# A two-layer sequence kernel on one core: the scaling of expert results moved to ScalarE, one expert's weight splitting spread over the first expert stage, and the choice of experts moved within a range

## The reference, cut to what matters

```
x = layernorm(x + L0_attn(x))      # 16 heads of 8, band |i-j| <= 16, softmax; plus residual
x = layernorm(x + L0_ffn(x))       # 16 experts 128->512->128, gelu, the 4 best by logits, softmax weights
x = layernorm(x + L1_attn(x))      # linear attention: decayed causal sum, reads @ W_read.T
x = layernorm(x + L1_ffn(x))       # 8 experts, silu(g)*u, the 2 best
# L0_ffn, the part that the change touches:
logits = -dist2 + einsum(x, rw) + rb;  topv, topi = top_k(logits, 4);  w = softmax(topv)
fused  = sum(w[..., None] * sel, axis=2)          # sel: the 4 chosen experts' outputs of a row
```

## Time and profile before

| | |
|---|---|
| three runs | 998.93, 1001.55, 1002.11 us; median 1001.55 us |
| the profiled execution | 1000.16 us, its span 998.3 us |
| mean granted TensorE clock | 0.852 |
| busy share of the span | PE 74%, PEld 60%, DVE 66%, ACT 49%, POOL 55% |
| chain that ended last | PE 62%, DVE 11%, POOL 9%, issue 8%, ACT 5%, DMA 3% |

### The profile page before, as it was taken

The page is one execution under the profiler, slowest core; times in us unless marked ns, Lnnn a source line. Parts: engine busy times, 40 slices in busy tenths (PEclk is TensorE's granted clock), DMA queues, the critical chain, the costliest instruction groups (busy, mean ns, idle before and its releaser), DMA issues.

```text
span 998.3 us, 34845 instructions
## 1 busy us (share of the span) xinstructions
PE 733.8 (74%) x11638; PEld 599.3 (60%) x11639; DVE 654.9 (66%) x1995; ACT 488.2 (49%) x1174; POOL 545.2 (55%) x562
## 2 busy tenths in 40 slices
PE   2789889789987109999999982656664189999900
PEld 0466566566666108899999881545543179899900
DVE  3456667577667407777777775777785367777756
ACT  1455557357555107666666650223322257777713
POOL 1022185486577755777776771377677624444433
PEclk9599999899999559999999995766676589999955
DMA  7011021121222233434444423233332233222253
GB/s 220 2 46 30 26 78 48 47 81 52 62 72 87 78 108 77 81 79 88 87 84 88 87 56 126 77 106 103 116 107 63 85 65 65 64 55 53 51 166 97
DMA packets 135794, 78.97 MB, mean 79 GB/s; under 512 B 104338, under 2 KB 116793, under 8 KB 135696
## 3 DMA queue, kind: packets, MB, share of 16 engines
q1 hardware_dynamic: 121808, 50.97, 20.9%
q0 software_dynamic: 13312, 25.31, 8.1%
q10 hardware_dynamic: 576, 1.34, 0.4%
HBM read 32.34 MB, written 32.63 MB: 65 GB/s over the span
## 4 chain that ended last, share of the span: by engine, by line
PE 62%; DVE 11%; POOL 9%; issue 8%; ACT 5%; DMA 3%; SPq 0%; POOLq 0%; DVEq 0%; ACTq 0%
PE avbank L1707 8%; PE proj L1707 7%; POOL xs L639 7%; PE avbank L1558 5%; PE s L1686 3%; PE s L1687 3%; PE s L1688 3%; PE t L1686 3%; PE t L1687 3%; PE t L1688 3%; PE t L1752 3%; PE t L1545 2%; PE s L1508 2%; PE proj L1464 2%; DVE nm L795 2%
## 5 line engine op out<-in xcount | busy, mean ns | idle before, releaser
L705 POOL DMA_INDIRECT yt<-ysb,to_now x224 | 231.7, 1035 | 160.5 <-ACT ysb L1335 87.4
L639 POOL DMA_INDIRECT xs<-x1p,sidx x192 | 189.0, 984 | 60.3 <-issue 48.0
L935 DVE CAST h_hi<-act_out 128x512 bf16<-128x512 f32 x152 | 71.1, 468 | 75.6 <-ACT act_out L1348 70.2
L1686 PE MATMUL s<-xt,w_hi 128*128 128x256 bf16 x296 | 81.8, 276 | 41.4 <-DMA xt<-xs 41.4
L936 DVE TENSOR_TENSOR h_lo<-act_out,h_hi 128x512 bf16<-128x512 f32 x152 | 106.4, 700 | 5.2
L1249 ACT ACTIVATE prob<-t 128x384 f32<-128x384 f32 (+1 forms) x160 | 73.2, 511 | 36.3 <-PE t L1545 36.0
L622 POOL TENSOR_TENSOR w_lo<-w_raw,w_hi 128x512 f32 (+1 forms) x28 | 32.5, 1160 | 106.8 <-ACT w_hi L1319 106.6
L1687 PE MATMUL s<-xt,w_hi 128*128 128x256 bf16 x296 | 81.9, 277 | 0.0
L1688 PE MATMUL s<-xt,w_lo 128*128 128x256 bf16 x296 | 81.9, 277 | 0.0
L1707 PE MATMUL avbank<-w_hi,h_hi 128*128 x448 | 81.0, 220 | 1.0 <-issue 0.6
L1686 PE MATMUL t<-xt,w_hi 128*128 128x256 bf16 x296 | 81.5, 275 | 0.0
(11 more groups left out here) (233 smaller groups left out, 2049.7 us busy)
## 6 DMA issues: line engine op xcount, KB each, us to landing
w_raw<-w_all SPq DMA_DIRECT2D x56, 256.0 KB
gat<-yt SPq DMA_DIRECT2D x8, 1024.0 KB, 6.0
gat<-yt SPq DMA_DIRECT2D x8, 512.0 KB, 4.2
yt<-ysb,to_now POOLq DMA_INDIRECT x224, 2.3
xs<-tail_rows SPq DMA_DIRECT2D x24, 129.0 KB, 2.2
xs<-x1p,sidx POOLq DMA_INDIRECT x192, 2.7
out<-ow SPq DMA_DIRECT2D x8, 256.0 KB, 2.3
xt<-xs SPq DMA_TRANSPOSE x112
```

The lines of the kernel that those rows point to most:

```text
L639: pool.indirect_dma_start(out=xs[n][:, :], out_offset=bass.IndirectOffsetOnAxis(sidx[:, par, at:at + 1], 0), in_=x1p[:, par, t, k, :], in_ ...
L705: pool.indirect_dma_start(out=yt[n][:, :], out_offset=bass.IndirectOffsetOnAxis(to_now[:, u, s:s + 1], 0), in_=ysb[:, u, s, :], in_offset= ...
L935: ch.link(dve.tensor_copy(h_hi[:, par, c, :], act_out[:, par, c, :]))
L1686: pe.matmul(dst, w_h, xt[:, u, 0, :], start=True, stop=False)
```

## The change

It has four parts.

1. **Prologue.** ScalarE's load of `cb` is issued after the first input (`loaded_x`) has landed, and a one-element exponential stands ahead of it. SP also waits for `loaded_x` before its later loads.
2. **Attention.** For range b−1, `choose` and `mark` move from w = 4 to w = 3, and `weigh`, `take_ranks`, `place`, PE's `ranks` and ScalarE's `route`, `spread` and `keep` from w = 0 of the next body to w = 4. The paced scatters stand in windows 0 to 3 instead of 1 to 4.
3. **Expert stage 0.** One chunk of the second block's weights is loaded, copied and subtracted for each group of four tiles (16 groups), so that one chunk a range is left for the linear stage.
4. **Linear stage.** `combine` (16 multiply-adds of 128x128 for a range on DVE) becomes 16 scalings of 128x128 on ScalarE in place (`scale_results`), and on DVE one addition of 128x1024 (`pair_up`) and two of 128x512 (`add_up`). `x2_apply` moves behind `x1f`, PE's `turn_x1` ahead of `turn_x2`, and `logits` ahead of the first `write_scores`. `FIRST` is 3.

```diff
-            with sp.Fori(1, CHUNKS_0 // 2 + 1) as c:
+            with sp.Fori(1, CHUNKS_0 // 2) as c:
...
+                    if n == 0:
+                        load_weights(g)
...
-                        if prev == 2 and w > 0:
-                            if (w, g) == (1, 0):
+                        if prev == 2 and w < T:
+                            if (w, g) == (0, 0):
...
-                scatter(0, par, w - 1, (g,))
+                scatter(0, par, w, (g,))
...
-            FIRST = 5
+            def low_weights(b, par):
+                pool.wait_ge(hi_done, CHUNKS_0 + b + 1)
+                pool.tensor_tensor(w1_lo[:, bass.ds((GROUPS_0 + b) * CH, CH)], w_raw[:, par, :],
+                                   w1_hi[:, bass.ds((GROUPS_0 + b) * CH, CH)], ALU.subtract).then_inc(lo_done, 1)
+            FIRST = 3
...
-                for k in range(CPB_1):
-                    low_weights(b, i, par, k)
+                low_weights(b, par)
...
+                            if u == 2:
+                                dve.wait_ge(hi_beside, g + 1)
+                                apart(dve)
+                                dve.tensor_tensor(w1_lo[:, bass.ds(g * CH, CH)], w_raw[:, 0, :],
+                                                  w1_hi[:, bass.ds(g * CH, CH)], ALU.subtract).then_inc(lo_beside, 1)
...
-            def combine(n, b, count, par, ks):
-                k_n = top[n]
-                if 0 in ks:
-                    ch.link(dve.tensor_copy(wsel[:, :, :], wres[:, bass.ds(b * T, T), 0:k_n]))
-                    dve.wait_ge(gathered[n][par], 16 * count)
-                for k in ks:
-                    for t in range(T):
-                        before = xres[:, b * T + t, :] if k == 0 else y[:, t, :]
-                        ins = dve.scalar_tensor_tensor(out=y[:, t, :], in0=gat0[:, par, t, k, :],
-                                                       scalar=wsel[:, t, k:k + 1], in1=before,
-                                                       op0=ALU.mult, op1=ALU.add)
-                    if k < k_n - 1:
-                        ch.link(ins)
-                    else:
-                        ins.then_inc(comb_done, 1)
-                        dve.wait_ge(comb_done, B * n + b + 1)
+            def add(dst, a, other):
+                return dve.scalar_tensor_tensor(out=dst, in0=a, scalar=1.0, in1=other, op0=ALU.mult, op1=ALU.add)
+            def pair_up(b, par):
+                dve.wait_ge(weighted_in, b + 1)
+                ch.link(add(gat0[:, par, :, 0:2, :], gat0[:, par, :, 0:2, :], gat0[:, par, :, 2:4, :]))
+            def add_up(b, par):
+                ch.link(add(y[:, :, :], gat0[:, par, :, 0, :], xres[:, bass.ds(b * T, T), :]))
+                add(y[:, :, :], gat0[:, par, :, 1, :], y[:, :, :]).then_inc(comb_done, 1)
+                dve.wait_ge(comb_done, b + 1)
...
                 stats(lambda t: y3[:, t, :], stat3, mv3, ve3, var3_ready)
-                if nxt:
-                    x2_apply(b + 1)
                 if prev == 2:
                     dve.wait_ge(scattered1[par], 16 * T * K1 * i)
                 if not prev:
@@ -1008,14 +1015,16 @@
                     ins = dve.tensor_scalar(x1f[:, t, :], y3[:, t, :], mv3[:, t, 0:1], rstd3[:, t:t + 1],
                                             ALU.subtract, ALU.mult)
                 ins.then_inc(x1_ready, 1)
+                if nxt:
+                    x2_apply(b + 1)
                 if nxt2:
-                    combine(0, b + 2, i + 2, par, (0, 1))
-                if nxt:
-                    decay_of(b + 1, 0)
+                    pair_up(b + 2, par)
+                    add_up(b + 2, par)
                 take_logits(1, b)
...
-                        if w == 0 and prev == 2:
-                            beside = lambda: take_ranks(0, b - 2, rk_ps)
+                        if w == 4 and prev:
+                            beside = lambda: take_ranks(0, b - 1, rk_ps)
                         divide(win - 1, (w - 1) % NW, par if w > 0 else 1 - par, beside)
...
                         if prev:
                             take_logits(0, b - 1)
-                        if not nxt:
                             choose(0)
                             mark(0)
                     if w == 4 and nxt:
                         for g in range(G):
                             max_of(b + 1, 0, g)
                         split_max(b + 1, 0)
-                        if prev:
-                            choose(0)
-                            mark(0)
-                    if w == 4 and not nxt:
+                    if w == 4 and prev:
                         weigh(0, b - 1)
-                        take_ranks(0, b - 1, last_rk_ps)
                         place(0, b - 1, 1 - par)
...
+            act.wait_ge(v_zero, 1)
+            nc.scalar.activation(decay_m[:, 0:1], vf[:, 0, 0, 0, 0:1], ACT.Exp)
             act.wait_ge(loaded_x, 16 * LOADS_X)
+            act.dma_start(cb[:, :], const_b).then_inc(loaded_act, 16)
...
-                    if w == 4 and not nxt:
+                    if w == 4 and prev:
                         route(0, b - 1)
-                        spread(0, b - 1, 1 - par)
                     probs(win, w, 2)
                     probs(win, w, 3)
                     if w == 4 and nxt:
                         values(b + 1, 1 - par)
-                    if w == 0 and prev == 2:
-                        route(0, b - 2)
                     if w == 0 and nxt:
                         half(b + 1, 0)
                     if w == 1:
@@ -1309,17 +1309,15 @@
                         lay_max(win + 1, 0)
                     if w == 0 and nxt:
                         half(b + 1, 1)
-                    if w == 0 and prev == 2:
-                        spread(0, b - 2, par)
-                        keep(b - 2)
+                    if w == 4 and prev:
+                        spread(0, b - 1, 1 - par)
+                        keep(b - 1)
...
+                        if n == 0 and u == 1:
+                            act.wait_ge(raw_in_beside, 16 * g + 16)
+                            apart(act)
+                            nc.scalar.copy(w1_hi[:, bass.ds(g * CH, CH)], w_raw[:, 0, :]).then_inc(hi_beside, 1)
...
+            def scale_results(b, at, use):
+                act.wait_ge(gathered[0][at], 16 * use + 16)
+                for t in range(T):
+                    for k in range(K0):
+                        ins = nc.scalar.activation(gat0[:, at, t, k, :], gat0[:, at, t, k, :], ACT.Identity,
+                                                   scale=wres[:, bass.ds(b * T + t, 1), k:k + 1].rearrange("p a k -> p (a k)"))
+                ins.then_inc(weighted_in, 1)
...
+                act.wait_ge(x1_turned, B + b + 1)
+                nc.scalar.copy(x1_tl[:, :], xbank[:, :]).then_inc(x1_copied, 1)
                 if nxt:
                     keep_x2_turned(b + 1)
-                act.wait_ge(x1_turned, B + b + 1)
-                nc.scalar.copy(x1_tl[:, :], xbank[:, :]).then_inc(x1_copied, 1)
                 high_rows(1, b, i, par)
-                for k in range(2):
-                    high_weights(k)
+                high_weights()
                 spread(1, b, par)
                 route(1, b)
                 keep(b)
                 if nxt:
                     keep_values(b + 1)
-                high_weights(2)
+                if nxt2 == 2:
+                    scale_results(b + 3, 1 - par, i + 2 if par else i + 1)
...
-                if nxt:
-                    turn_x2(b + 1)
                 pe.wait_ge(rank_used[1], b)
                 turn_x1(1, b, xbank)
                 if nxt:
+                    turn_x2(b + 1)
+                logits(1, b, rt_lg)
+                if nxt:
                     pe.wait_ge(x2_copied, b + 2)
                     write_scores(b + 1, 0)
-                logits(1, b, rt_lg)
                 if nxt:
                     for e in range(1, T):
                         write_scores(b + 1, e)
```

More of the change, by code:

```diff
@@ L82 @@
 TILES = max_tiles(E0, K0)
+GROUPS_0 = B * L * K0 // (RING * TILE)
+assert CHUNKS - CHUNKS_0 - GROUPS_0 == B and TILES // RING <= CHUNKS - CHUNKS_0
 FIN = 4
@@ L353, in program @@
         scaled = sem("scaled")
+        weighted_in = sem("weighted_in")
+        raw_in_beside, hi_beside, lo_beside = sem("raw_in_beside"), sem("hi_beside"), sem("lo_beside")
         scattered1 = pair_of("scattered1_")
@@ L513, in numbers_of, with load_weights @@
                     load_numbers(row, u)
+                def load_weights(g):
+                    if not (type(g) is int and g == 0):
+                        sp.wait_ge(lo_beside, g)
+                        apart(sp)
+                    sp.dma_start(w_raw[:, 0, :], w_all[:, bass.ds(g * CH + CHUNKS_0 * CH, CH)]).then_inc(raw_in_beside, 16)
                 def group(g):
@@ L548, in _ @@
                     load_outputs(0, b + 2)
-                for c in range(CHUNKS_0 + CPB_1 * b + 2, min(CHUNKS_0 + CPB_1 * (b + 1) + 2, CHUNKS)):
```

(31 more changed lines are left out.)

45 lines of the change are left out of this document (16 added, 29 removed).

## The result

The changed kernel takes 991.2 us (median of four runs, 989.63 to 991.82) against 1001.59; the ratio is 0.9905, 95% interval 0.9883 to 0.9927. Its profiled run took 991.68 us, its span is 989.8. The forecast was 989.8 in a range of 977 to 999. The sum came out; several of its terms did not, and they hid each other: between the two profiled executions the stages give −8.5 us where the forecast had −11.2. That the median lies within 1.4 us of the forecast is partly luck.

The account below looks back on a forecast made before the run. The order in POOL's program, not engine work, bounds the linear stage. Terms −3.5 + 1 − 2.5 + 0.3 + 3.1 − 9.6 = −11.2 give 989.0 from the profiled 1000.16, 990.4 from the median; forecast 989.8, range 977 to 999.

Parts of the forecast that it names:

- Prologue (−3.5): Prologue: later `cb` load saves 2.5 us, table load off the path 1.28, later loads cost 0.3; sum −3.5.
- Attention (+1): Attention loop: `ranks` and `take_ranks` ahead of the reciprocal +3.1 us, `spread` and `keep` leaving w = 0 −2.3; sum +1.
- Rival 2: Attention: `spread` and `keep` before the exponentials delay TensorE 2.4 us in seven ranges; total +5.4, 1007 us; chance 0.05.
- Tail (−2.5): Scatter tail after attention: range 6's first scatter starts near 321.6, not 324.07, limited by its place numbers; −2.5 us.
- Stage 0 (+0.3): Expert stage 0: added copies on ScalarE and subtractions on DVE fit into free time; +0.3 us, bounds 0 and +3.
- rival 5: Expert stage 0: 16 DVE subtractions held up 0.73 us each beside POOL, TensorE waiting; +12 us, 1001.5; chance 0.03.
- Head (+3.1): Head of linear stage: 16 scalings at 0.32 us, then additions, replace `combine` before TensorE's first turn; +3.1 us.
- Linear stage (−9.6): Linear stage: period falls by 1.65 us to 19.0, −9.9 in six ranges; range 0 +1.0, last range −0.7.
- two scatters: Linear stage: two scatters fewer ahead of the power for the norm; −2.46 us a range.
- the chunks: Linear stage: scatters wait for the place numbers and no longer for the third weight chunk; −0.5 us a range.
- rival 4: Linear stage: shorter pause keeps TensorE at its upper clock, −4.1 us a range, 961 us; chance 0.07.
- Rivals 1 and 3: Linear stage: 1, period stays at 20.3, 998 us, chance 0.11; 3, slow scalings make ScalarE the bound, 1026, chance 0.02.

Follow-up runs that it names:

- e7: Changed kernel, but POOL's subtraction for the weight chunk alone waits for the mask of chosen experts; the rows' subtraction does not; 977.1 us, single run.
- e11: Changed kernel with all 24 weight chunks split in the linear stage again, three a range, none beside expert stage 0; 1008.37 us (1.0102).
- e8: Changed kernel with POOL's subtractions waiting for the mask, and range 0 summed on DVE by 16 multiply-adds, ScalarE scaling from range 1; 976.94 us (0.9763).
- e1: Changed kernel where POOL waits for the mask of chosen experts before subtracting the low part of rows and weight chunk; 982.63 us (0.9818).

## Why the prediction was right, and where it was not

- **Prologue (−3.5).** Right in the trace (−3.9) and alone (−3.5, by the interval 1.4 to 4.9). Both mechanisms are seen: statistics at 6.8, no table load ahead of `xn_t`.
- **Attention (+1).** Wrong in sign: −1.8 in the two traces, −4.6 on the mean of all profiles. The forecast counted for `ranks` and `take_ranks` "two to three such instructions, +0.45 us in seven ranges": the new wait, and not the one that it replaces. In w = 0 of before, DVE waited 1.22 us for the same ranks (its instruction at 225.68), ahead of the next reciprocal; in the new place it waits 0.54 (at 212.74). This is worth little, as the stretches at full clock show. The larger miss is that the sum held no term for the clock in attention, though its windows stood in the profile. Rival 2 did not come: TensorE waited 1.8 us in all for `prob` in attention against 3.4 before, and behind the moved `spread` and `keep` 0.61 us, at the start of the last range.
- **Tail (−2.5).** −0.1 in the two traces, yet other profiles bear the term out: from last `xn_t` to last scatter the new order takes 101.5 us in e7, 2.5 less than before, and 102.3 in the middle of its ten profiles. In the changed kernel's profile the place numbers of range 6 came 60.77 us after the last `xn_t` at a clock of 0.94, against 58.66 at 0.97 before (58.68 at 1.00 in e7), and POOL waited for them. So the two misses of −2.8 and +2.4 cancelled in this pair of profiles by chance.
- **Stage 0 (+0.3).** +0.6 to +0.9 in the nine profiles that split chunks there, and 0 in e11; inside the bounds. The traces show 19 subtractions there, one for each four of the 76 tiles, and not the 16 of the forecast; each takes 0.68 or 0.69 us, so rival 5 did not come there.
- **Head (+3.1).** +3.2, with the scaling at 0.295 and not 0.32; e8 shows that it was avoidable.
- **Linear stage (−9.6).** −7.5. The chain was as written up to the logits, but the period fell by 1.03 and not 1.65. Here is the step that failed: the forecast gave this place no term for POOL and DVE side by side. Rival 5 named the mechanism, in the wrong stage: POOL's subtractions hold up a two-input instruction of DVE. Behind five scatters instead of three they start 2.2 us later against the powers, just when `dtop` is due. Of the −7.5, six periods give −6.2, range 0 gives +0.6 (forecast +1.0) and the last range −2.0 (forecast −0.7). Without the hold the period is 18.61, better than the forecast's 19.0. The terms inside were off as well: two scatters 1.9 and not 2.5; the scaling +1.3 and not 0; the chunks 2.4 and not 0.5, since the three edits need each other.
- **Expert stage 1** ended 0.8 us later than the linear stage's lead; other runs show 0.1 to 1.4. The cause is open.
- The clock in the linear stage stayed low in the burst (0.50 in 688 to 692), so rival 4 did not come. Rivals 1 and 3 did not either.

## What to carry to other kernels

Look at a moved instruction not only for what it waits for, but for what now runs beside it on the other engines: a two-input DVE instruction of 0.2 us took up to 2.7 us, 0.9 of them paid in each range, and one wait on the other engine gave about 6 us back. When parts of a change are priced one by one, test them one by one as well: here a sum that fitted to 1.4 us held one part, attention with its tail, that was off by 3 to 6. And look at the granted clock of each stretch before and after a change of order: a stretch in which it fell was 1.1 to 2.8 us longer here, where the pauses ahead of the falls were 0.6 to 1.35 us long.

## What the runs showed of the hardware that was not expected

- DVE's `dtop` is recorded as held from before POOL's subtraction is recorded to start (693.48 against 693.87; in e7 683.78 against 684.17), while a scatter alone does not hold it: in e1 one runs from 687.63 to 688.59, and `dtop` at 688.22 takes 0.17 us. POOL's second subtraction is recorded to start 0.05 us before the first one ends (694.98 against 695.03), and DVE does not get in between: it stays held over both. The Trainium skill, page "SBUF — State Buffer", section "Who interferes with whom", has the contention of a DVE instruction with two inputs in SBUF and a GpSimd instruction that reads SBUF; the traces agree.
- A pause of TensorE of 1.29 to 1.33 us in a stage at full clock was followed by a fall of the clock to 1.2 GHz in five of six cases (in before by 3 us at a granted 0.50); behind 0.95 or 0.96 us in the same place of the new order the clock stayed at 2.4 GHz in 26 of 30.
- The same attention program took from 241.8 to 245.3 us in ten profiles, while the runs of one kernel differ by 2 to 6 us here.
